# Layer 0's filter spectra on TensorE: the first into the middle of the second projection, the second behind the gate's bias product

## The chip, the cores and the metric

The kernel runs on one core of a Trainium2 chip. The metric is the time of one execution on the device, in microseconds (us). The kernel before was run three times; the profile is of one further execution.

## What is computed

The input x is 128 graphs of 128 nodes and 256 features, adj a sparse 128 x 128 matrix for each graph. Two layers follow one another, both with a residual and a layer norm. The change lies in layer 0:

```python
in_degrees = jnp.sum(adj, axis=-1)
norm = jnp.power(in_degrees + 1e-06, -0.5)[..., None]
f_hom = jnp.einsum('bnd,de->bne', x, theta) * norm
f_hom = jnp.einsum('bnm,bmd->bnd', adj, f_hom) * norm
f_het = jnp.einsum('bnd,de->bne', x, W_h)
gate = jax.nn.sigmoid(jnp.einsum('bnd,de->bne', x, W_t) + b_t)
out = gate * f_hom + (1.0 - gate) * f_het
# x = layernorm(x + elu(out))
```

Layer 1 has a convolution over the nodes with 17 taps (conv2_w, 256 x 256 x 17), message sums and a GRU. The kernel does that convolution in the frequency domain, and so it needs the spectrum of each filter. These spectra depend on the weights alone and are made during layer 0.

## The kernel before

The kernel runs in stages, each of which ends in a barrier: layer 0 with the filter spectra (phase_a), the spectrum of layer 1's convolution input, its product with the filters, and the rest of layer 1. The change is in TensorE's part of phase_a.

**Units and steps.** phase_a takes the graphs in 64 pairs. Each engine runs a software pipeline that is written out in full (written_out, L53): at step i an engine works on unit i - s in its part of stage s, if live(s) says that this unit exists. All engines have a step function of their own, and the order inside it is the order of their instructions. They meet through semaphores alone; reached(engine, semaphore, count) is a wait.

**Precision.** Each float32 operand is split into a high and a low part in the fp32r type, and a product is three matmuls: low by high, high by low, high by high. With two chunks of features that makes the six entries of terms (L575).

**TensorE's step before (L601 to L645), in order:**
1. the degrees: four matmuls with 2 columns (L604, L605) into ps_t, which wait for al, the low part of adj that GpSimd makes (L433)
2. project(0): six matmuls of 512 columns (L595), x by theta and W_h for the first graph of the pair, into ps_hh
3. the fourth filter spectrum of the filter group before, spectra(t - 7, 3)
4. the messages of unit i - 3: six matmuls of 256 columns (L616) into ps_hom, "hom" below
5. the first filter spectrum, spectra(t - 6, 0)
6. project(1): six matmuls of 512 columns for the second graph
7. the second filter spectrum, spectra(t - 6, 1)
8. four transposes of x1 of unit i - 7 (L632) into ps_t
9. the bias product (L638), a matmul of 512 columns into ps_g, and behind it the gate: twelve matmuls of 256 columns (L641)
10. the third filter spectrum, spectra(t - 6, 2)

**A filter spectrum** (spectra, L577 to L587) is one matmul of 272 columns with 102 rows into ps_w, a bank of which there is one. Before it, TensorE waits on s_gw until ScalarE has copied the spectrum before it out of that bank (spectra_out, L319 to L326, which waits on s_gm for the matmul). The first of four also waits on s_gs for the stacked taps, which SP loads (L268). t is i + 4, so the filters run ahead of the units.

**The bias product's wait.** L637 waits on s_gd: the gate's bank ps_g is free only when VectorE has read it into gd (L532) for the unit before. gd in turn waits for diff (L525), and diff for the end of hom (s_hom). VectorE's order in a step is: the degrees' sums (L505), y and its statistics (L509 to L518), diff, gd, mix (L535), fl (L541), x1 (L548), and in every fourth step the low part of the taps (L559).

**ScalarE's order in a step** is: below and ex (L343, L346), the fourth spectrum's copy, xh (L354), ah (L356), fh of the first graph (L317), the first spectrum's copy, in every fourth step the high part of the taps (L367), fh of the second graph, het (L371), the second spectrum's copy, x1t (L378), the gate's tanh (L381), the third spectrum's copy. The steps 18, 20 and 22 carry a copy of constants besides. GpSimd's order is: the roots (L416), xl (L421), res (L428), al (L433).

**SP** loads the inputs four units ahead, moves the taps, and stores the finished filter spectra to DRAM (L276) and x1 (L285).

Of the kernel before, what the change touches and what calls it, by code (L numbers as in the profile page):

```python
# [31 lines left out]
def reached(eng, sem, count):  # L32

    if isinstance(count, int) and count <= 0:
        return
    eng.wait_ge(sem, count)
# [16 lines left out]
def written_out(units, stages, step, unroll, lead=0):  # L53

    for i in range(-lead, units + stages - 1):
        step(i, i % unroll, i // unroll, lambda s, i=i: 0 <= i - s < units)
# [14 lines left out]
def phase_a(nc, G, x_n, x_t, adj_t, w0, b_t, masks, x1_t, taps, taps_s, dft_w, w_spec, w_c1, bn1, dft_f, keep, s_spec, s_out, first_x, s_x):  # L71
# [16 lines left out]
    with ExitStack() as ctx:  # L88
# [133 lines left out]
        def taps_live(i):  # L222
            return lambda s: 0 <= i + LEAD - s < pairs
# [339 lines left out]
        @block.tensor  # L563
        def _(pe):
            pe.wait_ge(s_wl, 1)
            pe.wait_ge(s_wh, 2)
            pe.wait_ge(s_k, 5)

            def step(i, n, k, live):
                u = n % 2  # L570
                v = 1 - u
                t, tn, tk = i + LEAD, (i + LEAD) % UNROLL, (i + LEAD) // UNROLL
                ahead = taps_live(i)
                p2 = i - 2
                terms = [(xx, ww, c) for c in range(KD) for xx, ww in ((xl, w_hi), (xh, w_lo), (xh, w_hi))]  # L575

                def spectra(q, c):  # L577
                    r = q % RING
                    if c == 0:
                        reached(pe, s_gs[r], 16 * (q // RING + 1))  # L580
                    if q == 0 and c == 0:
                        pe.wait_ge(s_wl, 2)
                    if t == 18 + LEAD and c == 3:

                        pe.wait_ge(s_ch, 1)
                    reached(pe, s_gw, 4 * q + c)
                    nc.tensor.matmul(ps_w[:, 0:GW], gs[:, r, c], dw[:, :], start=True, stop=True).then_inc(s_gm, 1)  # L587

                def project(b):
                    if b == 0:  # L590
                        reached(pe, s_xl, p2 + 1)
                        reached(pe, s_fl, p2 - 1)
                        reached(pe, s_mix, p2 - 1)
                    for o, (xx, ww, c) in enumerate(terms):
                        last = nc.tensor.matmul(ps_hh[:, 2 * u + b, :], xx[:, u, c, b * P:b * P + P], ww[:, c, 0:2 * D],  # L595
                                                start=(o == 0), stop=(o == len(terms) - 1))
                    last.then_inc(s_proj, 1)

                if live(2):
                    reached(pe, s_al, p2 + 1)  # L600

                    reached(pe, s_x1t, i - 7)
                    for b in range(2):
                        nc.tensor.matmul(ps_deg[:, b], al[:, u, b], ones[:, 0:2], start=True, stop=False)  # L604
                        last = nc.tensor.matmul(ps_deg[:, b], ah[:, u, b], ones[:, 0:2], start=False, stop=True)  # L605
                    last.then_inc(s_deg, 1)
                    project(0)
                if ahead(7):
                    spectra(t - 7, 3)
                if live(3):  # L610
                    p = i - 3
                    reached(pe, s_fl, p + 1)
                    reached(pe, s_diff, p)
                    for b in range(2):
                        for o, (aa, ff) in enumerate(((al, fh), (ah, fl), (ah, fh))):
                            last = nc.tensor.matmul(ps_hom[:, b], aa[:, v, b], ff[:, v, b], start=(o == 0), stop=(o == 2))  # L616
                    last.then_inc(s_hom, 1)
                if ahead(6):
                    spectra(t - 6, 0)
                if live(2):  # L620
                    project(1)
                if ahead(6):
                    spectra(t - 6, 1)
                if live(7):
                    p = i - 7
                    reached(pe, s_x1, p + 1)
                    reached(pe, s_x1t, p)

                    reached(pe, s_dege, p2 + 1 if live(2) else pairs)
                    for b in range(2):  # L630
                        for c in range(KD):
                            last = nc.tensor.transpose(ps_t[:, c, b * P:b * P + P], x1[:, v, b, c * P:c * P + P], ident[:, :])  # L632
                    last.then_inc(s_xp, 1)
                if i == 2:
                    pe.wait_ge(s_wl, 6)
                if live(2):
                    reached(pe, s_gd, p2)  # L637
                    nc.tensor.matmul(ps_g.rearrange("p b d -> p (b d)"), ones[:, :], bt_rows.rearrange("p b d -> p (b d)"), start=True, stop=False)  # L638
                    for b in range(2):
                        for o, (xx, ww, c) in enumerate(terms):  # L640
                            last = nc.tensor.matmul(ps_g[:, b], xx[:, u, c, b * P:b * P + P], ww[:, c, 2 * D:3 * D],  # L641
                                                    start=False, stop=(b == 1 and o == len(terms) - 1))
                    last.then_inc(s_gp, 1)
                if ahead(6):
                    spectra(t - 6, 2)  # L645

                if i == 17:

                    pe.wait_ge(s_gw, 4 * (t - 6) + 3)
                    pe.wait_ge(s_cn, 7)  # L650
                    nc.tensor.matmul(ps_w[:, 0:D], ones0[:, :], diag[:, 0].rearrange("p c n -> p (c n)"), start=True, stop=True)
                    nc.tensor.matmul(ps_w[:, D:2 * D], ones0[:, :], diag[:, 1].rearrange("p c n -> p (c n)"), start=True, stop=True).then_inc(s_bc, 1)

            written_out(pairs, STAGES, step, UNROLL, LEAD)


# [1266 lines left out]
```

## Time and profile before

| what | us |
|---|---|
| median of 3 runs | 1946.61 |
| lowest and highest run | 1945.92, 1946.75 |
| the profiled execution, its own time | 1950.68 |
| its span, first to last instruction | 1948.9 |
| TensorE busy, of the span | 1883.5 (97%) |
| VectorE busy | 1430.8 (73%) |
| ScalarE busy | 1114.8 (57%) |
| GpSimd busy | 424.5 (22%) |

The profile is of one execution of the program. Times in its rows are counted from the first instruction. PE is TensorE's matmuls and PEld its loads of stationary weights, which run beside matmuls; DVE is VectorE, ACT ScalarE, POOL GpSimd, SP the engine whose queue issues transfers. L587 is line 587 of the kernel. The end of a matmul is modelled, its start is recorded. Layer 0's stage runs from the start to about 463 us.

### The profile page before, as it was taken

The page shows a single profiled execution, that of the slowest core. Times are in us where ns is not written, and L with a number is a line of the kernel's source. Part 1 is how long each engine was busy: PE and PEld are TensorE (multiplying, and loading weights), DVE is VectorE, ACT ScalarE, POOL GpSimd, SP SyncE. Part 2 cuts the span into 40 slices and gives each one's busy share as a digit, 9 for nine tenths or more (in the row PEclk, how much of TensorE's full clock was granted, in tenths as well). Part 3 has the DMA queues.
Part 4 walks back from the last instruction along what each step waited for, and adds up shares of the span by engine and source line. Part 5 has one row for each costly group of instructions (what it writes and reads, how often), then busy time and mean ns, then how long its engine had stood idle before and what let it go on. Part 6 is the DMA issues. An engine that isn't in the chain of part 4 may idle for free.

```text
span 1948.9 us, 35045 instructions
## 1 busy us (share of the span) xinstructions
PE 1883.5 (97%) x11046; PEld 1655.4 (85%) x11046; DVE 1430.8 (73%) x2972; ACT 1114.8 (57%) x2063; POOL 424.5 (22%) x378
## 2 busy tenths in 40 slices
PE   7999999996999899969999999999999999999997
PEld 6989999996999799968888888888888888888886
DVE  5888888885666788866777777777777777777774
ACT  6888888884666677744444444444444444444442
POOL 4766766674444100000000000000000000000000
PEclk9999999997999899969999999999999999999999
DMA  6778888875334698852121212112121212121200
GB/s 219 268 271 289 289 293 296 310 248 195 97 101 132 197 291 280 272 182 91 51 102 51 93 58 84 67 62 89 50 101 50 101 50 96 55 88 64 79 33 22
DMA packets 184169, 281.13 MB, mean 144 GB/s; under 512 B 14286, under 2 KB 126644, under 8 KB 179860
## 3 DMA queue, kind: packets, MB, share of 16 engines
q1 hardware_dynamic: 184084, 280.10, 42.7%
q8 instruction: 41, 0.67, 0.1%
q14 instruction: 44, 0.36, 0.1%
HBM read 178.60 MB, written 101.45 MB: 144 GB/s over the span
## 4 chain that ended last, share of the span: by engine, by line
PE 54%; issue 1%; DVE 1%; ACT 0%; POOL 0%; POOLq 0%; ACTq 0%; DVEq 0%
PE c_ps_g L1660 40%; PE c_ps_m L1638 5%; PE c_ps_m L1669 2%; PE c_ps_y L1693 1%; PE c_ps_y L1703 1%; PE c_ps_m L1671 1%; PE c_ps_m L1703 1%; PE c_ps_m L1670 1%; PE c_ps_m L1704 0%; PE c_ps_y L1704 0%; PE c_ps_s L1697 0%; PE c_ps_s L1719 0%; PE c_ps_g L1722 0%; ACT c_yo L1342 0%; DVE c_stats L1578 0%
## 5 line engine op out<-in xcount | busy, mean ns | idle before, releaser
L1393 POOL TENSOR_TENSOR c_rstd<-c_var_eps,c_neg_half 128x4 f32<-128x4 f32 x32 | 32.2, 1008 | 1056.1 <-DVE c_var_eps L1586 1056.1
L1342 ACT ACTIVATE c_yo<-c_ps_y,c_shift,c_rstd 128x256 f32<-128x256 f32 x128 | 61.9, 565 | 168.5 <-DVE c_shift L1594 168.5
L1660 PE MATMUL c_ps_g<-c_nh,c_wi_l 128*128 128x512 f32 x384 | 153.5, 400 | 0.0
L1660 PE MATMUL c_ps_g<-c_ch,c_wi_l 128*128 128x512 f32 x384 | 153.1, 399 | 0.0
L1660 PE MATMUL c_ps_g<-c_xh,c_wh_l 128*128 128x512 f32 x384 | 152.4, 397 | 0.0
L1660 PE MATMUL c_ps_g<-c_xl,c_wh_h 128*128 128x512 f32 x384 | 152.3, 397 | 0.0
L1660 PE MATMUL c_ps_g<-c_xh,c_wh_h 128*128 128x512 f32 x384 | 152.1, 396 | 0.0
L1660 PE MATMUL c_ps_g<-c_nl,c_wi_h 128*128 128x512 f32 x384 | 151.9, 396 | 0.0
L1660 PE MATMUL c_ps_g<-c_nh,c_wi_h 128*128 128x512 f32 x384 | 151.8, 395 | 0.0
L1660 PE MATMUL c_ps_g<-c_cl,c_wi_h 128*128 128x512 f32 x384 | 150.7, 392 | 0.0
L1660 PE MATMUL c_ps_g<-c_ch,c_wi_h 128*128 128x512 f32 x384 | 150.6, 392 | 0.0
L940 PE MATMUL m_ps<-m_wh,m_xl 128*128 128x256 f32 (+1 forms) x406 | 131.7, 324 | 6.5 <-DVE m_wl L922 6.5
L940 PE MATMUL m_ps<-m_wl,s_x 128*128 128x256 f32 (+1 forms) x406 | 131.6, 324 | 0.0
L940 PE MATMUL m_ps<-m_wh,s_x 128*128 128x256 f32 (+1 forms) x406 | 130.7, 322 | 0.0
L416 POOL TENSOR_TENSOR a_roots<-a_sums_eps,a_neg_half 128x4 f32<-128x4 f32 (+1 forms) x68 | 91.4, 1344 | 89.2 <-DVE a_sums_eps L505 81.2
L325 ACT ACTIVATE a_spec<-a_ps_w 128x272 f32<-128x272 f32 x256 | 107.1, 418 | 2.3 <-PE a_ps_w L587 1.4
L595 PE MATMUL a_ps_hh<-a_w_hi,a_xl 128*128 128x512 f32 x256 | 107.0, 418 | 0.0
L733 POOL TENSOR_TENSOR s_xl<-s_x,s_xh 128x512 fp32r<-128x512 f32 x64 | 82.5, 1290 | 95.1 <-ACT s_xh L752 95.1
L595 PE MATMUL a_ps_hh<-a_w_hi,a_xh 128*128 128x512 f32 x256 | 101.7, 397 | 0.0
L595 PE MATMUL a_ps_hh<-a_w_lo,a_xh 128*128 128x512 f32 x256 | 100.6, 393 | 0.0
L1459 DVE SCALAR_TENSOR_TENSOR c_work<-c_ps_g,c_bi,c_work 128x512 f32<-128x512 f32 x64 | 48.1, 751 | 71.5 <-PE c_ps_g L1660 71.5
L421 POOL TENSOR_TENSOR a_xl<-a_xt,a_xh 128x512 fp32r<-128x512 f32 x64 | 84.0, 1312 | 64.7 <-ACT a_xh L354 64.7
(221 smaller groups left out, 6143.1 us busy)
## 6 DMA issues: line engine op xcount, KB each, us to landing
w_spec<-a_spec SPq DMA_DIRECT2D x32, 1088.0 KB, 8.6
m_w<-w_spec SPq DMA_DIRECT2D x34, 1024.0 KB, 8.0
a_xt<-in_x_t SPq DMA_DIRECT2D x64, 256.0 KB, 3.5
a_xn<-in_x_n SPq DMA_DIRECT2D x64, 256.0 KB, 5.3
x_t<-a_x1t SPq DMA_DIRECT2D x64, 256.0 KB, 5.0
s_x<-x_t SPq DMA_DIRECT2D x64, 256.0 KB, 3.0
y_spec<-x_spec SPq DMA_DIRECT2D x64, 256.0 KB, 5.7
c_x<-x_t SPq DMA_DIRECT2D x32, 512.0 KB, 4.1
```

Source lines behind the costliest of these rows:

```text
L325: nc.scalar.activation(spec[:, half, :, first:first + 2], ps_w[:, 0:GW].rearrange("p (d j) -> p d j", j=2), ACT.Copy).then_inc(s_gw, 1)
L416: nc.gpsimd.tensor_tensor(roots[:, u, these], sums_eps[:, u, these], neg_half[:, these], ALU.pow).then_inc(s_root, 1)
L421: nc.gpsimd.tensor_tensor(xl[:, v], xt[:, (n - 1) % RING], xh[:, v].bitcast(F32), ALU.subtract).then_inc(s_xl, 1)
L595: last = nc.tensor.matmul(ps_hh[:, 2 * u + b, :], xx[:, u, c, b * P:b * P + P], ww[:, c, 0:2 * D], start=(o == 0), stop=(o == len(terms) - 1))
L733: nc.gpsimd.tensor_tensor(xl[:, (u - 1) % 2], x[:, r], xh[:, (u - 1) % 2].bitcast(F32), ALU.subtract).then_inc(s_xl, 1)
L940: last = nc.tensor.matmul(out.rearrange("p r (q c) -> p r q c", q=CHUNKS), xx[:, v, c, part], ww[:, v, c].rearrange("p q r c -> p r q c")[ ...
L1342: nc.scalar.activation(yo[:, b], ps_y[:, b], ACT.Identity, bias=shift[:, b:b + 1], scale=rstd[:, b:b + 1]).then_inc(s_yo, 1)
L1459: nc.vector.scalar_tensor_tensor(npre[:, :], ps_g[:, IN_BANK[j], :], bi[:, 2, j:j + 1], hn[:, :], ALU.add, ALU.add).then_inc(s_np, 1)
L1638: last = nc.tensor.matmul(out, stationary, moving, start=(n == 0), stop=(n == len(passes) - 1))
L1660: last = nc.tensor.matmul(out, stationary, moving, start=(count == 0), stop=(count == total - 1))
L1669: nc.tensor.matmul(ps_inv[:, b], yh[:, b, cols], di[:, :, :], start=(b % 2 == 0), stop=False)
L1703: nc.tensor.matmul(both, mh[:, b, j * P:j * P + P], ahl[:, b].rearrange("p s n -> p (s n)"), start=True, stop=False)
```

## The change

TensorE's step function takes the first filter spectrum between the third and the fourth matmul of project(1), and the second filter spectrum between the bias product and the gate's matmuls. The order on all other engines, the waits inside spectra and the number of instructions stay. In the arms for a step that has only one of the two (ahead(6) without live(2)), the spectra are issued at their old places; both are true for i from 2 to 65, so these arms are never taken.

```diff
-                def project(b):
+                def project(b, between=None):
                     if b == 0:
                         reached(pe, s_xl, p2 + 1)
                         reached(pe, s_fl, p2 - 1)
                         reached(pe, s_mix, p2 - 1)
                     for o, (xx, ww, c) in enumerate(terms):
+                        if o == len(terms) // 2 and between is not None:
+                            between()
                         last = nc.tensor.matmul(ps_hh[:, 2 * u + b, :], xx[:, u, c, b * P:b * P + P], ww[:, c, 0:2 * D],
                                                 start=(o == 0), stop=(o == len(terms) - 1))
                     last.then_inc(s_proj, 1)
...
-                if ahead(6):
-                    spectra(t - 6, 0)
-                if live(2):
-                    project(1)
-                if ahead(6):
+                first_spectrum = (lambda: spectra(t - 6, 0)) if ahead(6) else None
+                if live(2):
+                    project(1, first_spectrum)
+                elif first_spectrum is not None:
+                    first_spectrum()
+                if ahead(6) and not live(2):
                     spectra(t - 6, 1)
...
                 if live(2):
                     reached(pe, s_gd, p2)
                     nc.tensor.matmul(ps_g.rearrange("p b d -> p (b d)"), ones[:, :], bt_rows.rearrange("p b d -> p (b d)"), start=True, stop=False)
+                    if ahead(6):
+                        spectra(t - 6, 1)
                     for b in range(2):
```

## Rows read from the trace of the kernel before

**Rows 1.** Busy time by stretch: us, busy and count of each engine, clock, DMA

```profile
60.00:440.00 380.00, 378.49 (x2433) 342.36 (x2433) 327.66 (x877) 328.50 (x752) 262.54 (x228) 1.00 0.82 284
449.00:473.00 24.00, 10.67 (x44) 8.90 (x45) 8.58 (x24) 5.92 (x10) 7.99 (x7) 0.50 0.83 307
```

**Rows 2.** The bias product's line: its loads, then who kept them waiting

```profile
L638 PEld LDWEIGHTS a_ps_g<-a_bt_rows,a_ones x64: 186/189/191, 19.8 to 443.4; 128*128 128x128 f32 x64
...
  DVE a_gd L532: 2.0, 5
```

**Rows 3.** Timeline of one settled step (i = 38), TensorE's weight loads: start, length

```profile
258.14 0.19 PEld L604 LDWEIGHTS a_ps_t<-a_ones,a_al 128*128 128x128 f32 x1
...
260.72 0.19 PEld L616 LDWEIGHTS a_ps_hom<-a_fh,a_ah 128*128 128x128 f32 x1
260.97 0.19 PEld L587 LDWEIGHTS a_ps_w<-a_dw,a_gs 102*128 102x128 f32 x1
...
263.05 0.19 PEld L638 LDWEIGHTS a_ps_g<-a_bt_rows,a_ones 128*128 128x128 f32 x1
...
264.82 0.19 PEld L604 LDWEIGHTS a_ps_t<-a_ones,a_al 128*128 128x128 f32 x1
```

**Rows 4.** The same step, TensorE's matmuls

```profile
260.84 0.28 PE L616 MATMUL a_ps_hom<-a_fh,a_ah 128*128 128x256 f32 x1
261.00 0.36 PE L587 MATMUL a_ps_w<-a_dw,a_gs 102*128 102x272 f32 x1
261.20 0.40 PE L595 MATMUL a_ps_hh<-a_w_hi,a_xl 128*128 128x512 f32 x1
261.45 0.40 PE L595 MATMUL a_ps_hh<-a_w_lo,a_xh 128*128 128x512 f32 x1
261.68 0.39 PE L595 MATMUL a_ps_hh<-a_w_hi,a_xh 128*128 128x512 f32 x1
...
263.07 0.48 PE L638 MATMUL a_ps_g<-a_bt_rows,a_ones 128*128 128x512 f32 x1
263.39 0.28 PE L641 MATMUL a_ps_g<-a_w_hi,a_xl 128*128 128x256 f32 x1
263.51 0.28 PE L641 MATMUL a_ps_g<-a_w_lo,a_xh 128*128 128x256 f32 x1
...
264.82 0.29 PE L587 MATMUL a_ps_w<-a_dw,a_gs 102*128 102x272 f32 x1
264.95 0.17 PE L604 MATMUL a_ps_t<-a_ones,a_al 128*128 128x2 f32 x1
```

**Rows 5.** The same step, ScalarE: start, length, [idle before it and releaser]

```profile
260.43 0.42 ACT L325 ACTIVATE a_spec<-a_ps_w 128x272 f32<-128x272 f32 x1
...
261.92 0.42 ACT L325 ACTIVATE a_spec<-a_ps_w 128x272 f32<-128x272 f32 x1
262.79 0.47 ACT L317 ACTIVATE a_fh<-a_ps_hh,a_roots 128x256 fp32r<-128x256 f32 x1 [0.45 <-PE a_ps_hh L595]
...
263.64 0.42 ACT L325 ACTIVATE a_spec<-a_ps_w 128x272 f32<-128x272 f32 x1
```

**Rows 6.** The same step, VectorE

```profile
261.22 0.88 DVE L525 SCALAR_TENSOR_TENSOR a_diff<-a_ps_hom,a_roots,a_het 128x256 f32<-128x256 f32 x2
262.24 0.69 DVE L532 SCALAR_TENSOR_TENSOR a_gd<-a_ps_g,a_diff 128x512 f32<-128x512 f32 x1
```

**Rows 7.** Timeline of an early step (i = 5): TensorE's matmul, VectorE, TensorE's load

```profile
37.39 0.28 PE L616 MATMUL a_ps_hom<-a_fh,a_ah 128*128 128x256 f32 x1
...
38.78 0.69 DVE L532 SCALAR_TENSOR_TENSOR a_gd<-a_ps_g,a_diff 128x512 f32<-128x512 f32 x1
...
39.52 0.19 PEld L638 LDWEIGHTS a_ps_g<-a_bt_rows,a_ones 128*128 128x128 f32 x1 [0.40 <-DVE a_gd L532]
```

**Rows 8.** Timeline of step 20, TensorE's first filter spectrum

```profile
140.55 0.36 PE L587 MATMUL a_ps_w<-a_dw,a_gs 102*128 102x272 f32 x1 [0.24 <-ACT a_spec L325]
```

**Rows 9.** The settled step of rows 3, GpSimd

```profile
263.94 0.73 POOL L433 TENSOR_TENSOR a_al<-a_at,a_ah 128x256 fp32r<-128x256 f32 x1
```

## The prediction

> **What bounds the kernel now.** I read the stages first. From 60 to 440 us, which is nearly all of layer 0, TensorE is busy for 378.49 of 380 us at full granted clock, while VectorE, ScalarE and GpSimd have room [rows 1]. So a step of this stage is a TensorE step. The bias product stands in it once: 64 times between 19.8 and 443.4 us [rows 2]. Then I read one settled step in time. TensorE's first degree load is at 258.14 us and the next one at 264.82, so a step takes 6.68 us [rows 3].
>
> A busy share near 100% hides short stalls, because the ends of matmuls are modelled and overlap. Starts are more honest. In this step the last message matmul (hom) starts at 260.84, the spectrum matmul behind it at 261.00 and the first projection matmul at 261.20 [rows 4]: 0.36 us for two matmuls. Elsewhere a 256-column one takes 0.12 (263.39 to 263.51) and a spectrum matmul 0.13 (264.82 to 264.95) [rows 4]. So 0.11 us is lost. The cause is the single spectrum bank ps_w: ScalarE copies the spectrum before out of it from 260.43 to 260.85 [rows 5], and only then may the next load go; it is at 260.97, 0.25 us after the one before it [rows 3]. This is the stall that the change takes away.
>
> The question is what is late next. The bias product writes ps_g, which VectorE reads for gd, so its load waits for gd. VectorE starts diff when hom has ended (261.22), and gd runs from 262.24 to 262.93 [rows 6]: 2.09 us from the start of the last hom matmul to the end of gd. The bias load is at 263.05 [rows 3], 0.12 us after gd. How small can that distance be? Early in the layer TensorE does wait there: 5 times, 2.0 us in all [rows 2]. In one of those steps hom starts at 37.39, gd ends at 39.47 (again 2.08 us later), and the load is at 39.52, 0.05 us after gd [rows 7]. So in a settled step the bias product is only 0.07 us (0.06 to 0.08 with rounding) from being held by gd, though the profile charges it with no wait there. That small slack decides this change.
>
> **The first spectrum, moved from behind hom into the middle of project(1).** Work between hom and the bias product is unchanged by this half alone; the stall of 0.11 goes. The copy it waits for ends at 260.85, and the matmul would now be reached behind three 512-column matmuls of 0.23 us each (261.45 to 261.68) [rows 4], near 261.65. Its own copy now starts at 261.92 [rows 5]; the matmul would end near 261.95 instead, so the copy slips by under 0.1 us. The next ScalarE instruction has waited 0.45 us for project(1) [rows 5], so that costs nothing in three steps of four; in the fourth a copy of taps stands in that gap, and VectorE's slack before diff takes the slip. SP's transfer of the stacked taps goes by the count of four steps back and is not near.
>
> **The second spectrum, moved from ahead of the transposes to behind the bias product.** TensorE reaches the bias load earlier by 0.11 (the stall) and 0.13 (this matmul): 0.24 us. It can use only 0.07 of that, since gd hangs on the end of hom and on two VectorE operations that nobody shortens. The other 0.17 us becomes a wait at the bias load. Behind it the moved matmul now stands on the path that was not waiting: bias, second spectrum, gate, third spectrum, degrees, project(0), fourth spectrum, hom, and again diff and gd. Nothing there has a gap to take it in. Its price is the spacing of its like: 0.12 us (a 256-column one) to 0.13 us (264.82 to 264.95); I take 0.13, as the same shape. For its own wait, the first spectrum's copy, there is room: that copy ends near 262.4 and the load comes near 263.1. Its copy on ScalarE now starts at 263.64 [rows 5]; the matmul would end 0.34 + 0.29 us after the bias load at 262.98, so at 263.61, no later than now. Queued behind it on ScalarE are the transposed x1, the gate's tanh and the third copy, all of which wait for the gate's end anyway or are not waited for soon.
>
> A page of the Trainium skill prices this matmul otherwise: "TensorE: Matmul & The Clock Gate", section "Back-to-back issue gap", gives N/2.4 + 2.5 ns for one at full clock, which would be an estimate of 0.116 us for 272 columns. By that the whole shift would come to about 3.1 us instead of 3.9. The rows show 0.13, so they disagree by 0.014 us per matmul, and the measured spacing is used.
>
> **The sum.** A settled step was 2.21 us (hom at 260.84 to the bias load at 263.05) plus 4.47 for the rest. Afterwards it is 2.14 + 4.47 + 0.13 = 6.74 us, 0.06 longer. Of the 64 steps:
> - 5 waited for gd already (their stall behind hom was hidden): 5 x 0.13 = 0.65 us.
> - 3 (i = 18, 20, 22) have a constant's copy on ScalarE, as the one with 0.24 us of idle at 140.55 [rows 8]. Their stall is larger and goes too, but al on GpSimd, made behind the same late ScalarE, then holds the next degrees; it has 0.15 us now (264.67 to 264.82) [rows 3, 9], so such a step can win 0.10 at most. I take -0.07 each, -0.2.
> - some 55 others: 55 x 0.062 = 3.4 us (0.13 less a slack between 0.06 and 0.07).
>
> Together +3.9 us. Bounds: 0.12 with slack 0.08 gives 55 x 0.04 + 0.6 - 0.2 = +2.6; 0.13 with slack 0.06 gives +4.3. Layers' later stages start behind the last step of this one (a barrier), so the shift is carried whole. The profiled execution took 1950.68 us (span 1948.9) and would take 1954.6; it stands 4.07 us above the median of 1946.61, so the median would be **1950.5 us**.
>
> **Rivals.**
> *The stall simply goes (faster).* That needs gd to come earlier by 0.17 us. Then TensorE would set the step at 6.57, but al, which ends at 264.67 [rows 9] for the load at 264.82 [rows 3], has 0.15 us, 0.10 beyond a delivery as gd's of 0.05, so at most 0.10 is won per step: 57 x 0.10 = -5.7, 1940.9 us. Against it: 2.08 and 2.09 us in two unlike steps say that VectorE starts on hom's end in both. Chance 0.07.
> *The moved matmul fits behind the bias product.* From the bias matmul's start to the gate's is 0.32 us (263.07 to 263.39) [rows 4] against 0.23 for other 512-column ones. If those 0.09 us were a gap, the matmul would cost 0.04 and a step would shrink by 0.03: 5 x 0.04 - 55 x 0.03 = -1.5 us, 1945.1. Against it: the 0.09 are the bias weights' load ahead of its stream, drawn into the start. Chance 0.10.
> *The moved matmul pays its load as well,* as the one behind hom did: 0.11 more per step, 64 x 0.11 = +7, 1957.5 us. Against it: its semaphore has long come, and a 512-column matmul runs while its weights load. Chance 0.05.
> *The later stages answer to the shift.* TensorE's granted clock was 0.50 (its 1.2 GHz level) from 449 to 473 us, when it was busy for 10.67 of 24 us in the drain of this stage [rows 1]. If a few microseconds of work fell on the other side of such a change, 1 to 2 us could come or go on top: 1948.5 to 1952.5. The three runs lie within 0.83 us, which speaks against much of it. Chance 0.08.
>
> **How the numbers follow.** The forecast has 0.70, with +2.6 to +4.3 us, 1949.2 to 1950.9. A measurement of this kernel can tell about 0.2%, 3.9 us, from no change, and the forecast sits on that line, so its chance is split: slower 0.37, same 0.33. To slower I add 0.05 (its load) and 0.05 of the later stages; to same 0.10 and 0.03; faster is the first rival, 0.07. That gives 0.47, 0.46 and 0.07. The range 1947.0 to 1952.5 takes in the forecast with its bounds, the clock case, and stops short of the two faster ones and the dear one.
>
> **What would show it.** In the trace of after: spectrum behind project(1)'s third matmul; hom's last start to the first projection start back to about 0.12; gd still 2.09 us after hom's start; the bias load 0.05 us after gd in every step, with some 0.17 us of idle put down to gd; a step of 6.74 us. A step of 6.58 with the bias load more than 0.05 behind gd would mean the first rival; a step of 6.65 with gd's wait present, the second. A last step shifted by 3.9 with another total would leave the later stages to look at.

## The result, and the profile after

The changed kernel takes 1951.32 us (median of 11 runs, 1950.07 to 1954.7) against 1945.96 us (median of 11, 1944.98 to 1949.17) for the kernel before on the same chip: ratio 1.0025, 95% interval 1.0017 to 1.0033. It is slower by about 4.9 us. The forecast was 1950.5 us and slower by 3.9.

The view of one line of the changed kernel, the bias product, gives the length of layer 0's stage from its first to its last load. Its first row answers to [rows 2]; its second row adds up the waits of the line's loads and of its matmuls.

```profile
L641 PEld LDWEIGHTS a_ps_g<-a_bt_rows,a_ones x64: 186/186/188, 19.9 to 447.7; 128*128 128x128 f32 x64
...
  DVE a_gd L532: 5.3, 10
```

The same 63 steps took 443.4 - 19.8 = 423.6 us before and take 447.7 - 19.9 = 427.8 us now: 4.2 us more. The second row is a lesson in reading. Its 10 waits are five steps, each counted once for its load and once for its matmul: the loads at 26.63, 33.35, 40.09, 46.83 and 101.30 us waited 3.7 us together, where the same five steps waited 2.0 us before [rows 2]. The rows below show a wait in a settled step that is not counted at all: the four transposes ahead of the bias product are drawn with 0.60 us from 264.99, to 265.59, which is past its start at 265.50. So the idle time by releaser is too small here, and starts must be compared.

TensorE's weight loads in a settled step, in the timeline of the changed kernel (start, length), to be laid beside [rows 3]:

```profile
260.66 0.19 PEld L606 LDWEIGHTS a_ps_t<-a_ones,a_al 128*128 128x128 f32 x1
...
263.23 0.19 PEld L618 LDWEIGHTS a_ps_hom<-a_fh,a_ah 128*128 128x128 f32 x1
263.35 0.19 PEld L597 LDWEIGHTS a_ps_hh<-a_w_hi,a_xl 128*128 128x128 f32 x1
...
264.77 0.58 PEld L635 LDWEIGHTS a_ps_t<-a_ident,a_x 128*128 128x128 f32 x4
265.50 0.19 PEld L641 LDWEIGHTS a_ps_g<-a_bt_rows,a_ones 128*128 128x128 f32 x1
...
267.41 0.19 PEld L606 LDWEIGHTS a_ps_t<-a_ones,a_al 128*128 128x128 f32 x1
```

The step is 267.41 - 260.66 = 6.75 us, where it was 6.68. The load behind the last hom load comes 0.12 us after it, where it took 0.25 [rows 3]: the stall is gone.

TensorE's matmuls of the same step, beside [rows 4]:

```profile
263.35 0.28 PE L618 MATMUL a_ps_hom<-a_fh,a_ah 128*128 128x256 f32 x1
263.47 0.40 PE L597 MATMUL a_ps_hh<-a_w_hi,a_xl 128*128 128x512 f32 x1
...
264.16 0.29 PE L587 MATMUL a_ps_w<-a_dw,a_gs 102*128 102x272 f32 x1
...
264.99 0.60 PE L635 MATMUL a_ps_t<-a_ident,a_x 128*128 128x128 f32 x4
...
265.84 0.29 PE L587 MATMUL a_ps_w<-a_dw,a_gs 102*128 102x272 f32 x1
265.97 0.28 PE L646 MATMUL a_ps_g<-a_w_hi,a_xl 128*128 128x256 f32 x1
```

VectorE and ScalarE in the same step, beside [rows 6] and [rows 5]:

```profile
264.75 0.69 DVE L532 SCALAR_TENSOR_TENSOR a_gd<-a_ps_g,a_diff 128x512 f32<-128x512 f32 x1
```

```profile
264.49 0.42 ACT L325 ACTIVATE a_spec<-a_ps_w 128x272 f32<-128x272 f32 x1
265.19 0.47 ACT L317 ACTIVATE a_fh<-a_ps_hh,a_roots 128x256 fp32r<-128x256 f32 x1 [0.28 <-PE a_ps_hh L597]
...
266.17 0.42 ACT L325 ACTIVATE a_spec<-a_ps_w 128x272 f32<-128x272 f32 x1
```

gd ends at 265.44, which is 2.09 us after the last hom matmul's start, as before, and the bias load follows 0.06 us later at 265.50. TensorE's loads for the four transposes are over at 264.77 + 0.58 = 265.35; then it waits. Behind the bias product the second spectrum takes 0.13 us (265.84 to 265.97). This step stands for all: over the whole stage the load lies 0.05 or 0.06 us behind gd's end in every one of the 63 steps behind the first, where before it lay 0.10 to 0.15 us behind it in most, and none of the last 40 steps takes less than 6.74 or more than 6.76 us. The time that was won behind hom went into the wait for gd, and the moved matmul came on top.

### The profile page after: what moved, and what is told of

Read it like the earlier page. It is cut to its first block, busy times and chain, and to the rows that moved or that the text cites. A ratio compares the mean times of both kernels' runs of the same rounds, so it can differ in the third digit from the quotient of the medians.

```text
span 1949.2 us, 35045 instructions
## 1 busy us (share of the span) xinstructions
PE 1883.1 (97%) x11046; PEld 1647.6 (85%) x11046; DVE 1428.4 (73%) x2972; ACT 1124.1 (58%) x2063; POOL 424.6 (22%) x378
## 4 chain that ended last, share of the span: by engine, by line
PE 54%; issue 1%; DVE 1%; ACT 0%; POOL 0%; POOLq 0%; ACTq 0%; DVEq 0%
PE c_ps_g L1665 40%; PE c_ps_m L1643 5%; PE c_ps_m L1674 2%; PE c_ps_y L1698 1%; PE c_ps_y L1708 1%; PE c_ps_m L1676 1%; PE c_ps_m L1708 1%; PE c_ps_m L1675 1%; PE c_ps_m L1709 0%; PE c_ps_y L1709 0%; PE c_ps_s L1702 0%; PE c_ps_s L1724 0%; PE c_ps_g L1727 0%; ACT c_yo L1347 0%; DVE c_stats L1583 0%
```

## The experiments

All are edits of the changed kernel unless it is said otherwise. "Stage" is the time from the first to the last load of the bias product in the profiled execution, the figure that was 423.6 before and 427.8 after. Ratios are against the kernel before on the same chip. Medians also hold differences of the granted clock, which the last section takes up, so the stage is the figure to compare.

**1. The first move alone.** The second spectrum goes back to its old place.

```diff
-                if ahead(6) and not live(2):
+                if ahead(6):
                     spectra(t - 6, 1)
...
-                    if ahead(6):
-                        spectra(t - 6, 1)
                     for b in range(2):
```

> The first spectrum in the middle of project(1), the second back at its old place behind project(1), ahead of the transposes. Theory (the bias product's load cannot come earlier than 0.05 us behind gd, 2.14 us behind the start of the last hom matmul, and the second spectrum costs 0.13 us only behind the bias product): nothing is added behind the bias product, so a settled step is 4.47 us plus the time from hom to the bias load. The second spectrum now comes right after project(1), while the copy of the first, which starts about 1.15 us after hom, ends at 1.57: TensorE waits about 0.08 us for it and reaches the bias load at about 2.17. Step 6.64 to 6.65 against 6.68 of before and 6.745 of both moves: about 2 us faster than before, 6 faster than both moves. Rival (splitting project(1) is what costs): a step near 6.75, as slow as both moves.

1945.71 us, ratio 0.9988 (0.9980 to 0.9997); stage 441.8 - 19.6 = 422.2 us. Two steps of its timeline:

```profile
254.67 0.69 DVE L532 SCALAR_TENSOR_TENSOR a_gd<-a_ps_g,a_diff 128x512 f32<-128x512 f32 x1
254.88 0.19 PEld L587 LDWEIGHTS a_ps_w<-a_dw,a_gs 102*128 102x128 f32 x1 [0.25 <-ACT a_spec L325]
...
255.45 0.19 PEld L641 LDWEIGHTS a_ps_g<-a_bt_rows,a_ones 128*128 128x128 f32 x1
...
262.10 0.19 PEld L641 LDWEIGHTS a_ps_g<-a_bt_rows,a_ones 128*128 128x128 f32 x1
```

The step is 6.65 us. The second spectrum's load waits for the first one's copy, as foreseen, and the bias load comes 0.09 us after gd's end (255.36), so that TensorE's own path ends last by a little. The first move is worth 1.4 us of stage by itself, and there is no sign that splitting the projection costs anything: the rival foresaw a step near 6.75 us.

**2. The second move alone.** The first spectrum goes back behind hom.

```diff
-                first_spectrum = (lambda: spectra(t - 6, 0)) if ahead(6) else None
+                if ahead(6):
+                    spectra(t - 6, 0)
                 if live(2):
-                    project(1, first_spectrum)
-                elif first_spectrum is not None:
-                    first_spectrum()
+                    project(1)
```

> The first spectrum back right behind hom, where it waits for ScalarE's copy; the second stays behind the bias product. Theory (gd's wait ends last): the stall of 0.11 us behind hom lies in the time that TensorE would wait for gd anyway, so it costs nothing: a step of 6.745 us as with both moves, the wait at the bias load about 0.06 instead of 0.17, 4 to 5 us slower than before. Rival (the first move already won its 0.11 and the second lost 0.18): a step near 6.85, 11 us slower than before.

1951.75 us, ratio 1.0021 (1.0012 to 1.0030); stage 447.0 - 19.2 = 427.8 us, the same as with both moves.

```profile
256.08 0.28 PE L618 MATMUL a_ps_hom<-a_fh,a_ah 128*128 128x256 f32 x1
...
256.43 0.39 PE L597 MATMUL a_ps_hh<-a_w_hi,a_xl 128*128 128x512 f32 x1
...
257.48 0.69 DVE L532 SCALAR_TENSOR_TENSOR a_gd<-a_ps_g,a_diff 128x512 f32<-128x512 f32 x1
258.22 0.19 PEld L640 LDWEIGHTS a_ps_g<-a_bt_rows,a_ones 128*128 128x128 f32 x1
...
264.95 0.19 PEld L640 LDWEIGHTS a_ps_g<-a_bt_rows,a_ones 128*128 128x128 f32 x1
```

The step is 6.73 us with the stall behind hom in place: 0.35 us from the last hom matmul to the first of the projection, for two matmuls. So the whole loss belongs to the second move, and in its company the first one is worth nothing: the stall of 0.11 us lies in time that TensorE would spend waiting for gd.

**3. The second spectrum ahead of the wait.** It goes behind the transposes but ahead of the bias product; the first one stays in the middle of project(1).

```diff
+                if ahead(6):
+                    spectra(t - 6, 1)
                 if i == 2:
                     pe.wait_ge(s_wl, 6)
                 if live(2):
                     reached(pe, s_gd, p2)
...
-                    if ahead(6):
-                        spectra(t - 6, 1)
```

> The first spectrum in the middle of project(1), the second behind the transposes and ahead of the bias product. Theory: the second spectrum again lies in front of gd's wait, and the four transposes give the copy of the first the time it needs, so there is no stall of TensorE's own; the bias load comes 0.05 us behind gd, 2.14 behind hom, and the step is 4.47 + 2.14 = 6.61 to 6.62. About 3.5 to 4 us faster than before, 8 faster than both moves. Rival (al on GpSimd or the split projection binds first): a step of 6.65 or more.

1942.99 us, ratio 0.9976 (0.9966 to 0.9986); stage 440.0 - 20.3 = 419.7 us.

```profile
254.85 0.19 PEld L641 LDWEIGHTS a_ps_g<-a_bt_rows,a_ones 128*128 128x128 f32 x1
...
259.31 0.28 PE L618 MATMUL a_ps_hom<-a_fh,a_ah 128*128 128x256 f32 x1
...
260.72 0.69 DVE L532 SCALAR_TENSOR_TENSOR a_gd<-a_ps_g,a_diff 128x512 f32<-128x512 f32 x1
...
261.47 0.19 PEld L641 LDWEIGHTS a_ps_g<-a_bt_rows,a_ones 128*128 128x128 f32 x1
```

hom to the bias load is 2.16 us here, gd's end (261.41) to the load 0.06. From the load at 254.85 in the step before it is 6.62 us, as foreseen. The two places of this one matmul stand a single instruction apart, one on either side of a wait, and the stage differs by 8.1 us: 0.13 us in each of 63 steps.

**4. A shorter way to gd.** From the second unit on this kernel leaves out diff of the second graph of each pair, so its output is not that of the layer; it serves for timing alone.

```diff
-                    for b in range(2):
+                    for b in range(2 if i == 3 else 1):
                         last = nc.vector.scalar_tensor_tensor(diff[:, b], ps_hom[:, b], roots[:, v, b:b + 1], het[:, v, b],
```

> Both moves as in the changed kernel, but VectorE computes diff for the first graph of a pair only (from the second unit on the second graph's diff is left out), so gd ends about 0.40 us earlier. Theory: TensorE then no longer waits for gd; next come TensorE's own work at 6.57 and al from GpSimd, which cannot come earlier than about 6.61 per step. Step 6.57 to 6.62, 7 to 10 us faster than the changed kernel and 3 to 6 faster than before. Rival (the moved matmuls cost by themselves, whatever gd does): step stays near 6.74.

1940.37 us, ratio 0.9966 (0.9955 to 0.9977); stage 438.5 - 20.5 = 418.0 us.

```profile
256.20 0.19 PEld L606 LDWEIGHTS a_ps_t<-a_ones,a_al 128*128 128x128 f32 x1
...
258.87 0.28 PE L618 MATMUL a_ps_hom<-a_fh,a_ah 128*128 128x256 f32 x1
...
259.93 0.69 DVE L532 SCALAR_TENSOR_TENSOR a_gd<-a_ps_g,a_diff 128x512 f32<-128x512 f32 x1
260.83 0.19 PEld L641 LDWEIGHTS a_ps_g<-a_bt_rows,a_ones 128*128 128x128 f32 x1
...
261.98 0.74 POOL L433 TENSOR_TENSOR a_al<-a_at,a_ah 128x256 fp32r<-128x256 f32 x1
262.62 0.19 PEld L587 LDWEIGHTS a_ps_w<-a_dw,a_gs 102*128 102x128 f32 x1
262.78 0.19 PEld L606 LDWEIGHTS a_ps_t<-a_ones,a_al 128*128 128x128 f32 x1
```

TensorE's program is that of the changed kernel, instruction for instruction; only VectorE has one operation less in a step. gd ends at 260.62, 0.21 us before the load, and the step falls to 6.58 us (256.20 to 262.78). gd was the bound. VectorE's other results for TensorE come earlier here too, but they did not bind: in the changed kernel fl ends at 267.07, 0.80 us ahead of project(0)'s first load at 267.87. The next bound shows at once: the degree load follows its predecessor by 0.16 us where 0.12 is the rule, held by al, which ends at 262.72, 0.06 us ahead of it. al was expected to allow no step below about 6.61 us; it allows 6.58.

**5. One matmul more, on either side of the wait.** The first spectrum's matmul is issued twice (ahead of the wait), or the second's (behind it):

```diff
                     reached(pe, s_gw, 4 * q + c)
+                    if c == 0:
+                        nc.tensor.matmul(ps_w[:, 0:GW], gs[:, r, c], dw[:, :], start=True, stop=True)
                     nc.tensor.matmul(ps_w[:, 0:GW], gs[:, r, c], dw[:, :], start=True, stop=True).then_inc(s_gm, 1)
```

> The changed kernel with the first spectrum's matmul issued twice in the middle of project(1) (same result). Theory: 0.13 us more ahead of the bias load, where TensorE now waits 0.17: a step stays at 6.74 to 6.76 and the time within 1 us of the changed kernel, the wait falls to 0.04. Rival (any matmul more costs its time, since TensorE is 97% busy): step 6.87, 8 us slower.

> The changed kernel with the second spectrum's matmul issued twice behind the bias product (same result). Theory: each matmul there costs its full spacing: a step of 6.86 to 6.88, 7.5 to 8.5 us slower than the changed kernel. Rival (part of a matmul fits into the start of the bias product): clearly less than 0.10 us per step.

Ahead of the wait: stage 448.2 - 20.5 = 427.7 us, nothing added by 64 matmuls. Behind it (c == 1): stage 454.4 - 19.3 = 435.1 us, 7.3 more, and 1961.0 us, ratio 1.0070 (1.0052 to 1.0088). One step of each, the one ahead first:

```profile
259.41 0.19 PEld L643 LDWEIGHTS a_ps_g<-a_bt_rows,a_ones 128*128 128x128 f32 x1
...
264.82 0.29 PE L588 MATMUL a_ps_w<-a_dw,a_gs 102*128 102x272 f32 x1
...
264.95 0.29 PE L589 MATMUL a_ps_w<-a_dw,a_gs 102*128 102x272 f32 x1
...
266.15 0.19 PEld L643 LDWEIGHTS a_ps_g<-a_bt_rows,a_ones 128*128 128x128 f32 x1
```

```profile
255.24 0.19 PEld L643 LDWEIGHTS a_ps_g<-a_bt_rows,a_ones 128*128 128x128 f32 x1
...
262.10 0.19 PEld L643 LDWEIGHTS a_ps_g<-a_bt_rows,a_ones 128*128 128x128 f32 x1
...
262.44 0.30 PE L588 MATMUL a_ps_w<-a_dw,a_gs 102*128 102x272 f32 x1
...
262.57 0.29 PE L589 MATMUL a_ps_w<-a_dw,a_gs 102*128 102x272 f32 x1
```

Steps of 6.74 and 6.86 us, as expected. One part of the expectation failed: the kernel with the twin ahead took 1955.36 us, ratio 1.0033 (1.0019 to 1.0047), not within 1 us of the changed kernel's 1951.3 or 1951.4. Its stage is no longer, so what it lost lies behind layer 0, and the last section shows that it goes with the granted clock.

**6. Three spectra ahead of the wait.** The fourth spectrum goes behind hom as well, the first behind the fourth matmul of project(1), the second goes ahead of the bias product as in experiment 3 (that part of the diff is not printed again); ScalarE's order follows, and its copy of the taps' high part moves from behind the first spectrum's copy to ahead of the fourth's.

```diff
-                if ahead(7):
-                    spectra(t - 7, 3)
                 if live(3):
                     p = i - 3
...
                     last.then_inc(s_hom, 1)
+                if ahead(7):
+                    spectra(t - 7, 3)
...
-                        if o == len(terms) // 2 and between is not None:
+                        if o == 4 and between is not None:
...
-                if ahead(7):
-                    spectra_out(t - 7, 3)
                 if live(1):
...
                     nc.scalar.activation(xh[:, v], xt[:, r], ACT.Copy).then_inc(s_xh, 1)
+                if ahead(1) and tn % TB == 1:
...
+                    nc.scalar.activation(th[:, :], tr[:, :], ACT.Copy).then_inc(s_th, 1)
+                if ahead(7):
+                    spectra_out(t - 7, 3)
+                if live(1):
...
-                if ahead(1) and tn % TB == 1:
...
-                    nc.scalar.activation(th[:, :], tr[:, :], ACT.Copy).then_inc(s_th, 1)
                 if live(2):
                     f_high(1)
```

> A version meant to beat both: the fourth spectrum behind hom instead of ahead of it, the first behind the fourth matmul of project(1), the second behind the transposes, the third last as before; on ScalarE xh and the taps' high part come ahead of the fourth spectrum's copy. Theory: three spectra now lie between hom and the bias load, so the path behind the wait is one matmul shorter than in second_ahead (4.34 + 2.14 = 6.49), al comes earlier too, and TensorE's own work of 6.57 is the bound: a step of 6.56 to 6.58, no wait for gd, about 6 to 7 us faster than before and 3 faster than second_ahead. Rival (the later copies of ScalarE make VectorE or TensorE wait): a step of 6.61 or more, no gain over second_ahead.

1940.45 us, ratio 0.9963 (0.9949 to 0.9977); stage 437.1 - 20.0 = 417.1 us. A step takes 6.55 us, but every fourth one 6.70, 13 steps in all. The wait for gd is gone from most steps, where the load comes 0.10 us or more behind gd's end; in one step of four it still comes 0.05 to 0.08 us behind, without making that step longer. What makes the 13 steps longer is ScalarE: its copy of the taps (start 250.70 in the timeline below) holds the fourth spectrum's copy and that holds the first spectrum's matmul:

```profile
251.50 0.39 PE L598 MATMUL a_ps_hh<-a_w_hi,a_xl 128*128 128x512 f32 x1
251.80 0.36 PE L588 MATMUL a_ps_w<-a_dw,a_gs 102*128 102x272 f32 x1
252.00 0.40 PE L598 MATMUL a_ps_hh<-a_w_lo,a_xh 128*128 128x512 f32 x1
```

```profile
250.70 0.64 ACT L357 ACTIVATE a_th<-a_tr 128x544 fp32r<-128x544 f32 x1
251.25 0.41 ACT L325 ACTIVATE a_spec<-a_ps_w 128x272 f32<-128x272 f32 x1
...
254.89 0.58 ACT L382 ACTIVATE a_ps_g<-a_ps_g 128x512 f32<-128x512 f32 x1 [0.48 <-PE a_ps_g L645]
```

0.50 us pass from the first to the last of these starts, where 0.36 would do (0.23 for the projection's matmul, 0.13 for the spectrum's); the missing 0.14 us is the longer step. The last row shows where ScalarE has 0.48 us free: ahead of the gate's tanh. So the copy of the taps was put there (the diff is against the version above):

```diff
                     nc.scalar.activation(xh[:, v], xt[:, r], ACT.Copy).then_inc(s_xh, 1)
-                if ahead(1) and tn % TB == 1:
...
-                    nc.scalar.activation(th[:, :], tr[:, :], ACT.Copy).then_inc(s_th, 1)
                 if ahead(7):
                     spectra_out(t - 7, 3)
...
                     nc.scalar.activation(x1t[:, v], ps_t[:, :, :], ACT.Copy).then_inc(s_x1t, 1)
+                if ahead(1) and tn % TB == 1:
...
+                    nc.scalar.activation(th[:, :], tr[:, :], ACT.Copy).then_inc(s_th, 1)
                 if live(2):
                     reached(act, s_gp, p2 + 1)
```

> three_ahead with the taps' high part (in every fourth step) moved on ScalarE from ahead of the fourth spectrum's copy to the idle time before the gate's tanh. In three_ahead a step took 6.55 us but every fourth one 6.70, since that copy held the fourth spectrum's and so the first spectrum's matmul. Theory: all steps come to 6.55 to 6.57, layer 0's stage gets 16 x 0.14 = 2.2 us shorter, 8 to 9 us faster than before in all. Rival (VectorE, with only 0.05 us of idle in those steps, is then the bound): every fourth step stays at 6.65 or more.

1937.44 us, ratio 0.9943 (0.9928 to 0.9959); stage 436.3 - 20.9 = 415.4 us, 12.4 less than the changed kernel and 8.2 less than the one before. That is 1.7 us less than the version before it, where 2.2 were expected from 16 long steps; there were 13. VectorE did not become the bound. This version computes the same and beats both. The ratio says more than the stage, 11 us, because all six executions had a granted clock of 0.985 or 0.986 and only 6 of the 16 of the kernel before had one. Those six have a median of 1945.81 us, 8.4 above this version, which is the 8.2 us of the stage.

**7. The changed kernel again.**

> The changed kernel once more, beside the version above and the kernel before on one chip, since twin_before_wait was measured in another job than the changed kernel. Theory: a settled step of 6.745 us, the last bias load 4.1 to 4.3 us later than in the kernel before, ratio 1.002 to 1.003; whatever the profiled executions differ in beyond that lies behind layer 0's stage, in stretches at the lower granted clock. Rival (part of the loss lies in the later stages): the stages behind layer 0 are longer than before at the same granted clock.

1951.44 us, ratio 1.0022 (1.0010 to 1.0035); stage 448.0 - 20.1 = 427.9 us, with settled steps of 6.75 us. The last bias load comes 4.6 us later than before, a little more than the 4.1 to 4.3 expected, since the first one comes 0.3 later too. The rival is not settled, for the kernel before has no profiled execution at the same granted clock, 0.986. From the last bias load to the end of the span it takes 1501.5 us here and 1499.1 to 1501.3 us in the six other versions that were profiled at 0.985 or 0.986.

## Why the prediction was right

- **The stall behind hom.** 0.11 us were to go; 263.35 to 263.47 is 0.12 where 0.36 stood for two matmuls. Right. That it buys nothing beside the second move is shown by experiment 2.
- **The slack of the bias product against gd.** The step of the prediction that decided, and the one that the profile's list of waits did not show. The distance from hom to gd's end stayed at 2.09 us, the load comes 0.05 or 0.06 us behind it in every step of the changed kernel but the first, and experiment 4, which shortens gd's way alone, takes the bound away. One of the signs named for it did not show: the profile puts no idle time down to gd in a settled step, though the wait is there.
- **The price of the moved matmul.** 0.13 us was taken; 265.84 to 265.97 says the same, and the two places of experiment 3 differ by 0.13 per step. A twin with the same weights and no wait of its own is a little cheaper: 7.3 us in 63 steps, 0.12. The estimate of 0.116 us for 272 columns, by the formula of the Trainium skill ("TensorE: Matmul & The Clock Gate", section "Back-to-back issue gap"), agrees with the twin and is too low for the moved matmul.
- **The sum.** +3.9 us was forecast, with 2.6 and 4.3 as bounds; the stage grew by 4.2, and by 427.9 - 423.6 = 4.3 in the repeat. The settled step was to be 6.74 and is 6.75 in the rows. The term that was off is the slack, taken a little too large: 0.07 was read from rows of two decimals, and 0.06 fits better. The five early steps were to give 0.65; the four intervals between their loads grew by 0.60 (26.37 to 26.97 us).
- **The three steps with a constant's copy.** al was to hold the degrees there. In step 20 the third spectrum's load and the degree load of the next step lie 0.33 us apart instead of 0.12, and al ends at 145.84, 0.05 us ahead of that load:

```profile
145.56 0.19 PEld L587 LDWEIGHTS a_ps_w<-a_dw,a_gs 102*128 102x128 f32 x1
145.89 0.19 PEld L606 LDWEIGHTS a_ps_t<-a_ones,a_al 128*128 128x128 f32 x1
```

```profile
145.09 0.75 POOL L433 TENSOR_TENSOR a_al<-a_at,a_ah 128x256 fp32r<-128x256 f32 x1
```

- **ScalarE's copies.** The first spectrum's copy was to slip by under 0.1 us against hom: 264.49 - 263.35 = 1.14, against 1.08 before. The second spectrum's was to be no later: 2.82, against 2.80. The idle time ahead of fh took the slip (0.28 left of 0.45). Right, and in the steps with a copy of the taps no step is longer either.
- **The rivals.** "The stall simply goes" fell: it needs gd earlier by 0.17 us. Its limit, al, was right in kind; with gd out of the way the step came to 6.58, which is what it named. "The matmul fits behind the bias product" fell with the 7.3 us of the twin and the 8.1 of experiment 3. "It pays its load as well" fell with 0.13. "The later stages answer to the shift" is not settled. What spoke against it was weak: the three runs lay within 0.83 us, but the kernel before took from 1943.91 to 1953.71 us in the sets of runs that followed.
- **What was not in the sum.** The measured difference is 4.9 us (3.3 to 6.4 by the interval), the stage's 4.2. In the set of experiment 7 executions of like granted clock can be compared: 1950.64 against 1945.81 us at 0.985 and above, 4.8 apart, and 1955.42 against 1950.71 below, 4.7 apart, for a stage that grew by 4.3. One of the rivals allowed 1 to 2 us for the later stages; whether the remaining 0.4 to 0.7 is theirs or noise, these runs cannot tell.
- **What was left to chance.** The forecast took the 4.07 us between the profiled execution and the median as an offset that stays. It did not: the changed kernel's profiled execution took 1950.99 us where 1954.6 were foreseen. The offset went with the granted clock, 0.981 in the profiled execution of the kernel before and 0.986 in that of the changed kernel. And the base was a median of three runs; that it stood within 0.7 us of the median of eleven was luck, not part of the argument.

## What to carry to other kernels

Before an instruction is moved, ask on which side of the wait that ends last it will stand: here one 0.13 us matmul cost 8 us on one side and nothing on the other, on an engine that is busy for 97%. A wait that the profile does not list can still be 0.06 us from binding, so measure the distance from the releaser's end to the waiting start and compare it with the same distance in a step that really waits. Taking out a stall pays only up to the next such distance, and the gain came when work went from behind the wait to ahead of it.

## What the runs showed of the hardware that was not expected

The part behind layer 0's stage is the same program in all these kernels, and its length still differed by 4 us between profiled executions. From the last bias load to the end of the span it took 1948.9 - 443.4 = 1505.5 us in the kernel before, 1949.2 - 447.7 = 1501.5 in the changed one, 1501.5 in its repeat, and 1953.9 - 448.2 = 1505.7 in the kernel with the twin ahead of the wait. The granted clock goes with it: its mean over the execution is 0.981 in the two long ones and 0.986 in the two short ones. Busy time by stretch (TensorE's granted clock is the number behind the last engine's count), the kernel before, then the changed one, then the one with the twin ahead:

```profile
840.00:900.00 60.00, 44.98 (x217) 38.46 (x216) 37.09 (x67) 23.65 (x33) 2.51 (x8) 0.74 0.37 123
```

```profile
840.00:900.00 60.00, 44.69 (x230) 38.49 (x229) 38.87 (x69) 24.72 (x35) 2.51 (x8) 0.83 0.40 134
```

```profile
840.00:900.00 60.00, 44.87 (x218) 38.50 (x218) 37.94 (x67) 24.74 (x34) 2.51 (x8) 0.74 0.48 159
```

Where layer 1's last stage begins, the clock averaged 0.74 or 0.83 of full speed; in these 60 us TensorE did 217 or 218 matmuls at 0.74 and 230 at 0.83. That accounts for only part of the 4 us. About half of it is there before that stage: ScalarE's last copy of the product with the filters starts 841.88 - 443.4 = 398.5 us behind the last bias load in the kernel before, and 844.03 - 447.7 = 396.3 us behind it in the changed one.

```profile
841.88 0.60 ACT L896 ACTIVATE x_spec<-m_ps 128x512 f32<-128x512 f32 x1 [0.84 <-PE m_ps L940]
```

```profile
844.03 0.60 ACT L901 ACTIVATE x_spec<-m_ps 128x512 f32<-128x512 f32 x1 [0.84 <-PE m_ps L945]
```

There too the clock differs: from 640 to 700 us it averaged 0.91 in the kernel before and 0.94 in the changed one. From 900 to 1940 us both have the full clock and do 5526 and 5524 matmuls. This is why the spans of the two profiled executions, 1948.9 and 1949.2 us, hide a stage that grew by 4.2 us: a difference between two single executions of this kernel must be read stage by stage.

The times of all executions say the same. Of the 22 of the changed kernel, the 13 with a mean granted clock of 0.985 or 0.986 took 1949.19 to 1951.81 us, and the 9 with 0.981 to 0.984 took 1952.39 to 1957.03. The kernel with the twin ahead had one at 0.985, 1952.33 us, and six at 0.981 to 0.983, 1953.28 to 1955.7: against executions of like clock it is not clearly slower, and its median of 1955.36 is that of the lower clock. Why a given execution gets the one clock or the other, and whether the order of the program has a part in it, stays open.
